# Mixing weights fetched in pairs behind the image stores, channel weights loaded by rows, and the other parameters moved later, in a Fourier layer tower

## The reference, cut to what matters

```python
h = layer_norm(x @ fc0_w + fc0_b, ln0_g, ln0_b)
for i in range(LAYERS):                      # 4, 32 channels, 12 x 12 modes
    w1 = w1r[i] + 1j * w1i[i]                # each part 32 x 32 x 12 x 12
    w2 = w2r[i] + 1j * w2i[i]
    x1 = spectral_conv(h, w1, w2)            # rfft2, mix channels per mode, irfft2
    x2 = einsum('bchw,oc->bohw', h, conv_w[i]) + conv_b[i]
    h = layer_norm(x1 + x2, ln_g[i], ln_b[i])
    if i < LAYERS - 1:
        h = gelu(h)
h = gelu(h @ fc1_w + fc1_b); h = gelu(h @ fc2_w + fc2_b); h = h @ fc3_w + fc3_b
```

## Time and profile before

| | |
|---|---|
| median of 3 runs | 3358.78 us (3358.08 to 3362.04) |
| profiled execution | 3361.34 us, its span 3359.6 us |
| busy in the span | PE 2941.6 us (88%), DVE 2141.6 (64%), ACT 1948.0 (58%) |
| mean granted clock of TensorE | 0.956 |
| moved by DMA | 335.91 MB, mean 100 GB/s |

### The profile page before, as it was taken

One profiled execution on the slowest core, in us unless ns is written; L12 is line 12 of the kernel. 1 busy time (PEld: TensorE's weight loads), 2 busy tenths in 40 slices (PEclk: granted clock), 3 DMA queues, 4 the chain that ended last, 5 costly groups with the idle time before them and its releaser, 6 DMA issues.

```text
span 3359.6 us, 82075 instructions
## 1 busy us (share of the span) xinstructions
PE 2941.6 (88%) x32240; PEld 1871.7 (56%) x32240; DVE 2141.6 (64%) x3949; ACT 1948.0 (58%) x2271; POOL 29.1 (1%) x17
## 2 busy tenths in 40 slices
PE   3888897999887999887999879999999987973994
PEld 2545465666665666655666644444444447961893
DVE  3888775888665888666888644444544444246457
ACT  3777664666554666554666547777777753432451
POOL 0000000000000000000000010000000001000000
PEclk7999999999998999999999999999999997996897
DMA  5222156444447444447444443111111000000000
GB/s 95 95 97 95 70 190 191 162 166 166 129 159 202 164 161 160 140 146 205 164 167 164 155 108 85 57 44 44 57 53 57 29 1 1 1 1 0 1 1 13
DMA packets 114157, 335.91 MB, mean 100 GB/s; under 512 B 45993, under 2 KB 78025, under 8 KB 78153
## 3 DMA queue, kind: packets, MB, share of 16 engines
q1 hardware_dynamic: 113992, 333.48, 30.8%
HBM read 179.29 MB, written 154.14 MB: 99 GB/s over the span
## 4 chain that ended last, share of the span: by engine, by line
PE 75%; DVE 10%; issue 5%; ACT 4%; SPq 3%; DMA 2%; DVEq 0%; ACTq 0%
PE pA L1286 14%; PE pA L1294 7%; PE pT L1380 7%; PE pT L1312 4%; PE pS L1323 4%; PE pD L1369 4%; PE pD L1337 4%; PE pD L1351 4%; PE pD L466 3%; PE pA L466 3%; PE pA L1276 2%; PE pD L1258 2%; DMA h_scratch<-h_new 2%; PE pS L458 2%; PE pT L458 2%
## 5 line engine op out<-in xcount | busy, mean ns | idle before, releaser
L1607 DVE TENSOR_REDUCE small<-arena 128x32 f32<-128x1056 f32 x320 | 396.8, 1240 | 353.4 <-ACT arena L1456 347.2
L1286 PEld LDWEIGHTS pA<-conv_bd,h_in 128*128 128x128 f32 x4096 | 478.8, 192 | 109.4 <-issue 92.7
L1286 PE MATMUL pA<-conv_bd,h_in 128*128 128x128 f32 x4096 | 517.1, 280 | 8.6 <-DVE arena L1600 3.0
L1446 ACT COPY w_sb<-pA 128x1024 f32<-128x1024 f32 x256 | 259.7, 1015 | 382.9 <-PE pA L1294 333.5
L1467 ACT ACTIVATE h_new<-pT,bet,gam 128x1024 f32<-128x1024 f32 x256 | 307.3, 1201 | 157.2 <-PE pT L1312 92.5
L1621 DVE SCALAR_TENSOR_TENSOR w_sb<-w_sb,small 128x1024 f32<-128x1024 f32 x320 | 386.6, 1212 | 5.5
L1456 ACT ACTIVATE arena<-w_sb 128x1024 f32<-128x1024 f32 x320 | 339.3, 1060 | 13.6
L1312 PE MATMUL pT<-cst,w_sb 128*128 128x128 f32 x2048 | 285.4, 284 | 64.1 <-ACT h_new L1467 43.0
L1312 PEld LDWEIGHTS pT<-cst,w_sb 128*128 128x128 f32 x2048 | 227.3, 144 | 185.5 <-issue 167.2
L1471 ACT COPY h_rows<-pS 128x1024 f32<-128x1024 f32 x256 | 256.9, 1004 | 66.1 <-PE pS L1323 66.1
L1323 PEld LDWEIGHTS pS<-cst,h_new 128*128 128x128 f32 x2048 | 228.8, 143 | 113.7 <-issue 71.9
(11 more groups left out here) (292 smaller groups left out, 3866.6 us busy)
## 6 DMA issues: line engine op xcount, KB each, us to landing
h_scratch<-h_new SPq DMA_DIRECT2D x128, 1024.0 KB, 4.2
h_in<-h_scratch SPq DMA_DIRECT2D x128, 1024.0 KB, 5.0
y_scratch<-w_sb SPq DMA_DIRECT2D x32, 576.0 KB, 8.8
y_in<-y_scratch SPq DMA_DIRECT2D x512, 36.0 KB
w_sb<-in_L_tok_w1r_dram SPq DMA_DIRECT2D x8, 576.0 KB, 11.5
w_sb<-in_L_tok_w1i_dram SPq DMA_DIRECT2D x8, 576.0 KB, 11.3
w_sb<-in_L_tok_w2r_dram SPq DMA_DIRECT2D x8, 576.0 KB, 18.0
w_sb<-in_L_tok_w2i_dram SPq DMA_DIRECT2D x8, 576.0 KB, 18.2
```

The source lines that it names most:

```text
L1286: pe.matmul(pA[:, c:c + 128], h_in[:, 1024 * n + c:1024 * n + c + 128], conv_bd[:], start=(j == 0), stop=False, skip_group_check=True)
L1607: dve.reduce_sum(var[n], sq[n % 2], axis=AX).then_inc(s["summed"], 1)
```

## The change

1. `weights` takes a slot and a half (w1 or w2) and makes two transfers instead of eight. It is called behind the second store of groups 1, 2, 3 and 4: slot 0 by groups 1 and 2, slot 1 by groups 3 and 4, in "first" for layer 0, in layer L for L+1. `y_store(L, 1)` also moves behind the stores of group 1 (the new argument `after` of `group`), and SP's wait for its landing behind group 4.
2. `cen.0` waits in body 3 for the four transfers of slot 0 (`128 * L + 64`), and in body 9 for all.
3. The channel weights are loaded by rows in four transfers, to a free place in `w_sb`, behind the stores of group 0, and are turned by one DVE transpose and put in place by four copies, in `conv_centre`.
4. The MLP parameters are loaded behind group 4 of "first", and the token parameters behind group 1 of "last" instead of group 0.

The diff:

```diff
--- before.py
+++ after.py
@@ -269,6 +269,7 @@
         TA = V.rearrange("p (h b c q) -> p b h c q", h=2, b=2, q=NQ)
         XF = [arena[:, 5152 + 768 * t:5920 + 768 * t] for t in range(2)]
         conv_all = arena[:, 7744:8256]
+        conv_rows, conv_cols = w_sb[:, 13312:13440], w_sb[:, 13440:13568]
         cbias = arena[0:C, 8256:8384]
         mlp = arena[:, 8384:8648]
         h_in = sb("h_in", [P, 4096])
@@ -357,7 +358,7 @@
         SLOTS = {"d": [pD[:]], "s": [pS[:]], "a": [pA[:]], "r": halves(pT)}
         names = ["d_full", "d_free", "s_full", "s_free", "a_full", "a_free", "r_full", "r_free", "acc_full", "conv_ready", "copied", "squared", "summed", "rooted", "root_chain",
                  "turned", "h_new_ok", "x_loaded", "y_loaded", "y_clear", "packed", "h_loaded0", "h_loaded1", "stored0", "stored1", "fc0_clear", "y_stored", "w_loaded",
-                 "w_centred", "mix_a_full", "mix_a_free", "mix_b_full", "mix_b_free", "y_bias", "conv_cleared", "conv_loaded", "conv_chain", "cst_loaded", "ln_loaded",
+                 "w_centred", "mix_a_full", "mix_a_free", "mix_b_full", "mix_b_free", "y_bias", "conv_cleared", "conv_loaded", "conv_turned", "conv_chain", "cst_loaded", "ln_loaded",
                  "fc0_loaded", "fc0_chain", "mlp_cleared", "mlp_loaded", "normed", "eps_set"]
         names += ["td_full", "td_free", "ts_full", "ts_free", "par_cleared", "par_loaded", "tok_ready", "v_chain", "shifted",
                   "exped", "e_subbed", "fc1_bias", "mlp_ready", "w1_split", "upper", "e_exped", "gated", "acc_done", "out_stored", "wg_scaled",
@@ -1004,22 +1005,19 @@
                 sp.wait_ge(s["h_new_ok"], at("h_new", ph, L, g, 2 * t + 2))
                 sp.dma_start(h_dram[g][:, c], h_new[:, c]).then_inc(s[f"stored{t}"], 16)
 
-            def weights(L):
-                for w, (wr, wi) in enumerate((("L0_tok_w1r", "L0_tok_w1i"), ("L0_tok_w2r", "L0_tok_w2i"))):
-                    for r in range(2):
-                        q = slice(64 * w + 32 * r, 64 * w + 32 * r + 32)
-                        for slot in range(2):
-                            name = wr if slot == r else wi
-                            sp.dma_start(w_v[q, slot].rearrange("p o m -> p (o m)"),
-                                         ins[name][L].rearrange("i o x y -> i (o x y)")).then_inc(s["w_loaded"], 16)
+            def weights(L, slot, w):
+                wr, wi = (("L0_tok_w1r", "L0_tok_w1i"), ("L0_tok_w2r", "L0_tok_w2i"))[w]
+                for r in range(2):
+                    q = slice(64 * w + 32 * r, 64 * w + 32 * r + 32)
+                    name = wr if slot == r else wi
+                    sp.dma_start(w_v[q, slot].rearrange("p o m -> p (o m)"),
+                                 ins[name][L].rearrange("i o x y -> i (o x y)")).then_inc(s["w_loaded"], 16)
 
             def conv_params():
+                for j in range(4):
+                    sp.dma_start(conv_rows[32 * j:32 * j + 32, :].rearrange("p (l c) -> p l c", l=LAYERS),
+                                 ins["L0_tok_conv_w"].rearrange("l o c -> o l c")).then_inc(s["conv_loaded"], 16)
                 sp.wait_ge(s["conv_cleared"], 1)
-                for L in range(LAYERS):
-                    for j in range(4):
-                        c = P * L + 32 * j
-                        sp.dma_start(conv_all[32 * j:32 * j + 32, c:c + 32],
-                                     ins["L0_tok_conv_w"][L].rearrange("o c -> c o")).then_inc(s["conv_loaded"], 16)
                 sp.dma_start(cbias, ins["L0_tok_conv_b"].rearrange("l o -> (l o)").partition_broadcast(C)).then_inc(s["conv_loaded"], 16)
 
             def mlp_params():
@@ -1090,7 +1088,7 @@
                 for dst, src in dmas:
                     sp.dma_start(dst, src).then_inc(s["par_loaded"], 16)
 
-            def group(ph, L, g, then=None):
+            def group(ph, L, g, then=None, after=None):
 
                 p = Phase(ph, L)
                 end = isinstance(g, int) and g == NG - 1
@@ -1117,36 +1115,41 @@
                 if ph != "last":
                     store_h(ph, L, g, 0)
                     store_h(ph, L, g, 1)
+                if after:
+                    after()
 
             def groups(ph, L):
 
-                def second_half():
-
-                    y_store(L, 1)
-                    weights(L + 1)
-
-                group(ph, L, 1, second_half if ph == "mid" else None)
+                to = 0 if ph == "first" else L + 1
+
+                def early(g):
+                    if ph == "mid" and g == 1:
+                        y_store(L, 1)
+                    weights(to, (g - 1) // 2, (g - 1) % 2)
+
+                for g in range(1, 5):
+                    group(ph, L, g, after=lambda: early(g))
                 if ph == "mid":
                     y_is_stored(L, 1)
-                with sp.Fori(2, NG - 2) as g:
+                else:
+                    mlp_params()
+                with sp.Fori(5, NG - 2) as g:
                     group(ph, L, g)
-                group(ph, L, NG - 2, lambda: y_store(0 if ph == "first" else L + 1, 0))
+                group(ph, L, NG - 2, lambda: y_store(to, 0))
                 group(ph, L, NG - 1)
 
-            weights(0)
-            conv_params()
-            mlp_params()
             sp.wait_ge(s["y_clear"], 1)
-            group("first", 0, 0)
+            group("first", 0, 0, after=conv_params)
             groups("first", 0)
             with sp.Fori(0, LAYERS - 1) as L:
                 group("mid", L, 0)
                 groups("mid", L)
             L = LAYERS - 1
-            group("last", L, 0, lambda: y_store(L, 1))
+            group("last", L, 0, after=lambda: y_store(L, 1))
+            group("last", L, 1)
             y_is_stored(L, 1)
             token_params()
-            with sp.Fori(1, NG - 1) as g:
+            with sp.Fori(2, NG - 1) as g:
                 group("last", L, g)
             sp.wait_ge(s["acc_done"], 1)
             sp.dma_start(out_ap.rearrange("(t b) y x -> (b y) t x", b=2), X.rearrange("p (t x) -> p t x", x=S)).then_inc(s["out_stored"], 16)
@@ -1533,7 +1536,15 @@
 
             def conv_centre():
 
-                dve.wait_ge(s["conv_loaded"], 16 * 17)
+                dve.wait_ge(s["conv_loaded"], 16 * 5)
+                dve.transpose(conv_cols, conv_rows).then_inc(s["conv_turned"], 1)
+                dve.wait_ge(s["conv_turned"], 1)
+                dve.wait_ge(s["conv_cleared"], 1)
+                for j in range(4):
+                    q = slice(32 * j, 32 * j + 32)
+                    dve.tensor_copy(conv_all[q].rearrange("p (l c) -> p l c", l=LAYERS)[:, :, 32 * j:32 * j + 32],
+                                    conv_cols[q].rearrange("p (l o) -> p l o", l=LAYERS)).then_inc(s["conv_turned"], 1)
+                dve.wait_ge(s["conv_turned"], 5)
                 cv, cb = conv_all.rearrange("p (x o) -> p x o", o=C), cbias.rearrange("p (l o) -> p l o", o=C)
                 dve.reduce_sum(cv_sum, cv, axis=AX)
                 dve.reduce_sum(cb_sum, cb, axis=AX).then_inc(s["conv_chain"], 1)
@@ -1575,7 +1586,11 @@
                 w = w_v[:, part, :, bass.ds(24 * i, 24)]
                 first = 18 * part + n
                 if n == 0 and part == 0:
+                    dve.wait_ge(s["w_loaded"], 128 * L + 64)
+                    alone(dve)
+                elif n == 0:
                     dve.wait_ge(s["w_loaded"], 128 * L + 128)
+                    alone(dve)
                 dve.wait_ge(s["w_centred"], 36 * L + first + 1 + 3 * i)
                 alone(dve)
                 if n == 0:
```

## The result

| | before | after |
|---|---|---|
| median of 16 runs | 3358.95 us | 3367.12 us |
| profiled execution's span | 3359.6 us | 3363.4 us |
| mean granted clock of TensorE | 0.956 | 0.952 |

The change makes the kernel slightly slower: the ratio is 1.0022, with a 95% interval of 1.0013 to 1.0031. The forecast was 3343, so it was wrong by 24 us, and the result lies outside its range. Some executions were disturbed (some 4% longer, at a lower granted clock): the medians of the changed kernel, of run 1 and of run 3 include two of sixteen, one of five and three of ten such, the ratios leave them out, the rows of runs 1, 3 and 9 come from disturbed executions and are read only up to 2000 us, where these are not yet slower, and of run 9 only one execution was undisturbed.

The account below looks back on a forecast made before the run. PE, busy 88% of the span, was taken to set the pace, with time to win where it stands still. Terms -33.0, +1.3, +13.5, -49.7 and +52.2 sum to -15.7 us, giving a median of 3343 us, range 3322 to 3356.

Parts of the forecast that it names:

- The start: Program start: x for group 1 is loaded early, so PE goes on near 30.5 us instead of 63.52; -33.0 us.
- The channel weights' +1.3: First phase: the added DVE transpose, four copies and waits, counted whole because PE waits for DVE; +1.3 us, bounds 0 and 3.4.
- What goes in the middle layers: Body 2 of each middle layer: its excess from the burst goes, 15.9 + 17.3 + 16.5; -49.7 us.
- Where the new stalls are: DVE waits for weights in body 3 of four phases, PE for y_in in middle layers; +13.5 and +52.2 us.
- rival E: Bodies 4 and 5: each of eight pairs gives its 5.5 us to PE, 44 more: 3387 us; chance 0.04.
- Rival B: Body 3, four places: DVE catches up, only 7.6 us lost at each, 20.5 less: 3323 us; chance 0.13.
- C: Weight and y transfers: pairs move at the full rate, 1.4 us less per 576 KB, 22 less: 3321 us; chance 0.03.
- F: Program start: something else holds PE at 30.5 and the 33 us stay: 3376 us; chance 0.03.
- The size of the new wait: DVE at cen.0, body 3: weights land 9.7 us after the store's issue; waits of 13.6 and 14.0 us.
- What the wait passes on: DVE's wait to PE, body 3: 12.5 us first phase, 12.8 per middle layer, each plus 1.0 for the clock.
- The y wait: Start of body 3, middle layers: y_in lands late and PE waits 3.6 us each time, bounds 0 and 6.
- Rival D: Middle layers: weights land after 12 us, y_in and h_in together 6 late, 16.4 more: 3359 to 3360 us; chance 0.14.

Follow-up runs that it names:

- run 1: The changed kernel with only DVE's order altered: cen.0 to cen.2 late in the body, all transfers where they were; 3450.35 us, 1.0266 of before.
- run 3: The changed kernel with the four y transfers of group 1 issued before the two stores of h again; 3351.77 us, 0.9970 of before.
- run 9: run 5 with cen.0 and cen.1 placed behind red.0, rs.0 and scale.0 in the middle layers only; 3309.25 us, in one execution.
- run 6: The changed kernel with y before group 1's stores, all four slot 0 transfers behind them, slot 1 in pairs behind groups 3 and 4; 3301.41 us, 0.9817 of before.
- Run 2: The changed kernel with the second pair of weight transfers issued before the stores of group 2 instead of behind them; 3308.79 us, 0.9856 of before.
- run 5: The changed kernel with the second weight pair before group 2's stores and the y transfers before group 1's stores; 3295.51 us, 0.9800 of before.
- run 8: The changed kernel with channel weights loaded by sixteen column transfers at their new place, without DVE's transpose and copies; 3370.43 us, 1.0023 of before.

## Why the prediction was wrong

- **The start: right.** For the first transposes -33.0 was forecast, -33.3 measured. The channel weights' +1.3 was measured as 1.34 us on DVE, and body 2 of the first phase is 1.3 us longer (26.0 for 24.7). Body 1 is 1.3 us shorter (23.1 for 24.4), which the prediction named as a bound ("It may be 1.5 us more") and left out of the sum.
- **What goes in the middle layers: right.** ACT's waits for the store went, and with them all of the 49.7 us.
- **Where the new stalls are: right.** They stand at the four bodies 3 and at the loads of `y_in`, and bodies 4 and 5 stay as they were (rival E fell). Rival B fell: DVE caught up nothing. C fell with the 2.9 us for each transfer in run 6, and F with the start.
- **The size of the new wait: the step that failed.** The prediction had "The landing of the weights is 4.2 (store) + 2 x 2.76 = 9.7 us after that" and so waits of 13.6 and 14.0 us; 16.13, 16.74, 17.93 and 17.73 were measured. The trace of layer 0 splits the 2.7 us that are missing there. DVE got to the instruction at 541.16 (557.90 - 16.74), and the store was issued 5.1 us behind that (546.24), where I had 4.3 from the earlier trace rows (571.1 - 566.83): PE begins this body after a pause and at a low clock (its first block takes 1.57 us, 0.91 in an ordinary body), and so `gelu.3` comes later. The weights landed 11.2 us after the store's issue instead of 9.7. And DVE began 0.5 us after the landing, for which I had nothing. In layers 1 and 2 the three parts are 6.0, 11.4 and 11.3, and 0.4 to 0.5; in the first phase 3.7, 12.0 and 0.4. The landing, the largest term of the three, can be read in its parts. First the store, then the last of the pair behind it (issued 0.9 us after it), each from its own issue; this view takes in the transfer before too, and the last of the pair is the 10.2:

```profile
L1006 SPq DMA_DIRECT2D h_scratch<-h_new x1: 343/343/343, 546.2 to 546.2; - x1
DMA to landing us min/median/max: 5.1/5.1/5.1
```

```profile
L1013 SPq DMA_DIRECT2D w_sb<-in_L_tok_w2i_dram x1: 827/827/827, 547.2 to 547.2; - x1
DMA to landing us min/median/max: 7.5/8.9/10.2
```

  The store took 5.1 us and not 4.2, and the pair the rest, 6.1 (547.15 + 10.2 - 551.3) and not 5.5. The 4.2 of the earlier trace rows is a median over all stores. In the changed kernel's trace a store of 1 MB landed after 3.9 us when nothing was issued for 10 us behind it (at 635.1), after 4.2 with loads of `y_in` 0.9 us behind it (at 645.5), and after 5.1 (5.05 to 5.11) in each of the thirteen cases with a pair of weight transfers 0.4 us behind it. I had taken the median for a queue that in my own plan had the pair in it.
- **What the wait passes on: the second part of the same step.** I let 1.2 us of each wait be absorbed in the middle layers and added 1.0 for the clock. Body 3 grew by 1.1 to 1.5 us more than DVE waited in the middle layers (17.8 for 16.74, 19.0 for 17.93, 19.2 for 17.73), and by 2.1 in the first phase (18.2 for 16.13). PE comes out of the pause at the lower level of its clock. Its matmuls of 64x512 (L1340) take 1020 ns each there and 600 in an ordinary body, and the granted clock (the number behind the engines' busy times, 0.78 and 1.00) says the same:

```profile
L1340 PE MATMUL pD<-h_rows,cst 64*32 64x512 f32 x32 | 3.8, 1020 | 2.6 <-DVE arena L1649 2.6
```

```profile
L1340 PE MATMUL pD<-h_rows,cst 64*32 64x512 f32 x32 | 2.2, 600 | 0.5 <-DVE arena L1649 0.5
```

```profile
561.00:581.00 20.00, 16.33 (x152) 7.94 (x153) 15.89 (x33) 7.12 (x8) 0.00 (x0) 0.78 0.20 71
609.00:629.00 20.00, 19.40 (x228) 13.84 (x209) 17.37 (x34) 13.19 (x14) 0.00 (x0) 1.00 0.62 163
```

- **The y wait: too small.** 3.6 us were forecast; PE waited 3.0, 5.2 and 5.3, and bodies 2 were 6.3, 4.9 and 5.0 too long. In layers 1 and 2 the pair behind y landed 30.0 and 30.6 us after the body's start (29.8 forecast), and PE began 2.5 and 2.1 us after that instead of 1.5. In layer 0, which began at the lower clock as in run 3, the store came 1.3 us later than forecast (10.4 us after the body's start instead of 9.1), and the pair took 6.7 us behind y instead of 5.5.

The sum of the errors: body 3 of the middle layers 56.0 against 3 x (12.8 + 1.0) = 41.4, bodies 2 16.2 against 10.8, the first phase 18.2 against 13.5. Together they are 24.7 us. The medians miss by 24 us, but that they agree so well is in part luck: the terms are read from the two profiled executions, and these miss by 19.5 (+3.8 measured, -15.7 forecast). Of the 5.2 us between, 1.6 are at the start and in body 1 of the first phase, and 3.3 come from the start of body 15 of layer 2 to the end (1452.9 us before, 1449.6 now). This last stretch takes 1444.5 to 1451.8 us in five other traces with the same steps in it, so its 3.3 us are not read as an effect of the change.

The mechanism was right, then, and its size was not. Rival D named this way (weights 12 us after the store, the loads 6 us late) and its terms were nearer (11.2 to 12.0 us, bodies 2 too long by 4.9 to 6.3), but it still came out 8 us short of the result, since it kept the forecast's time of the store's issue and its price for what a wait passes on. The deeper fault is in the balance. The forecast was a small difference of large terms (-82.7 against +67), and the new ones were computed from a median landing. The errors, 1.3 to 5.4 us at seven places, all had the same sign. The bounds that the range rests on, added with one sign, give 3327 to 3354: they had "a us either way" for waits that came out 2.5 to 3.9 us longer.

That a store and a wait could be arranged otherwise was in the prediction's own working: it says that two of the transfers "are issued behind the second store of group 2, and that store waits for `gelu.3`, in the same body 3". Run 2 takes just this away and gains 58 us.

Open is what PE waits for in the gaps that the profile ascribes to nothing. In bodies 2 and 3 of the middle layers, where weights are under way, they are 2.1 to 4.1 us long in runs 2, 3, 5, 6 and 8, and up to three in a run; neither the kernel before nor the changed one has one of over 2 us there. Open is also what of the landing of 11 to 12 us is due to the loads that SP issues behind the pair.

## What to carry to other kernels

When a burst is spread out, ask of every piece which compute step its issue is chained to: a transfer that sits in order behind a store cannot start before the step that the store waits for, and its consumer must be further from that step than store and transfer take together. Put what will be waited for first ahead of what is waited for later; here that order was worth 72 us, and the redistribution without it nothing. Before a waiting instruction is moved later instead, look at what it will then stand in front of in every iteration, since 0.4 us in each of 33 bodies cost as much here as 13 us of waiting in three. And where a forecast repeats one estimated term several times, its error repeats too, with the same sign: bound it by what the landing of a transfer can take with others around it, and add these bounds up.

## What the runs showed of the hardware

The issue time of a transfer on SP is no property of the transfer alone. The same sixteen loads of channel weights took 29.22 us of SP behind eight transfers of 576 KB, and 13.82 us in run 8, where only a store and nothing of that size stood ahead. A cost read in a full queue can't be carried to an empty one.

The landing time is no property of the transfer alone either. In the changed kernel's trace a store of 1 MB landed 3.9 us after its issue with nothing issued for 10 us behind it, 4.2 us with loads of 36 KB from 0.9 us behind it, and 5.1 us with a pair of 576 KB from 0.4 us behind it.
